# Products that nobody reads, in the gaps of TensorE's program behind the experts

## The reference, cut to what matters

```
h = layernorm(x) * (1 + ca) + sa
x = x + ga * L0_attn(h)      # convolutions, gated delta rule scan, output projection
h = layernorm(x) * (1 + cb) + sb
x = x + gb * L0_ffn(h)       # router, softmax gates over 8 experts of 128 -> 512 -> 128
h = layernorm(x) * (1 + ca') + sa'
x = x + ga' * L1_attn(h)     # in_proj, causal conv, state space scan in chunks, out_proj
h = layernorm(x) * (1 + cb') + sb'
x = x + gb' * L1_ffn(h)      # 128 -> 512, butterfly, gelu, butterfly, 512 -> 128
```

## Time and profile before

| | |
|---|---|
| median of 3 runs | 572.57 us (570.67 to 573.45) |
| profiled execution: its time | 571.0 us |
| its span | 568.9 us |
| PE busy in the span | 445.5 us (78%) |
| ACT / DVE / POOL busy | 392.6 / 376.6 / 193.0 us |
| mean granted clock of TensorE | 0.904 |

### The profile page before, as it was taken

The page is one execution under the profiler, slowest core; times in us unless marked ns, Lnnn a source line. Parts: engine busy times, 40 slices in busy tenths (PEclk is TensorE's granted clock), DMA queues, the critical chain, the costliest instruction groups (busy, mean ns, idle before and its releaser), DMA issues.

```text
span 568.9 us, 6438 instructions
## 1 busy us (share of the span) xinstructions
PE 445.5 (78%) x2064; PEld 303.8 (53%) x2064; DVE 376.6 (66%) x663; ACT 392.6 (69%) x661; POOL 193.0 (34%) x188
## 2 busy tenths in 40 slices
PE   5585597479975777998969989999999889864145
PEld 4474573267654654665746656676656566441012
DVE  1326958698979999799998958999231483022800
ACT  3798747757898558689745997746996676924242
POOL 0150961396108971048791104541003000030001
PEclk9988777978999999899988998999999999985557
DMA  7637537232270311800240081000000000000000
GB/s 204 231 122 180 164 100 300 47 93 75 67 140 1 93 40 56 188 0 1 60 109 0 1 189 38 1 1 1 0 1 20 1 1 1 0 18 0 1 1 18
DMA packets 35473, 36.49 MB, mean 64 GB/s; under 512 B 12904, under 2 KB 30832, under 8 KB 35184
## 3 DMA queue, kind: packets, MB, share of 16 engines
q1 hardware_dynamic: 35152, 31.88, 21.2%
q10 hardware_dynamic: 288, 4.19, 1.9%
HBM read 31.61 MB, written 3.28 MB: 61 GB/s over the span
## 4 chain that ended last, share of the span: by engine, by line
PE 34%; DVE 22%; ACT 16%; POOL 11%; issue 9%; DMA 2%; SPq 2%; POOLq 0%; DVEq 0%; ACTq 0%
PE psF L751 8%; PE psS L769 8%; PE psB L708 4%; DVE XX L1798 3%; DVE norm L1795 3%; DVE U L1815 3%; DVE T L1813 3%; DVE T L1817 3%; PE psM L812 3%; ACT L1086 2%; ACT hid L1280 2%; ACT L1088 2%; ACT hS L1129 2%; PE psM L819 2%; POOL G L2154 2%
## 5 line engine op out<-in xcount | busy, mean ns | idle before, releaser
L769 PEld LDWEIGHTS psS<-we2s,hid 128*128 128x128 f32 x1024 | 136.5, 196 | 61.2 <-issue 46.9
L751 PE MATMUL psF<-h,we1s 128*128 128x512 f32 (+1 forms) x320 | 139.7, 528 | 13.2 <-ACT hid L1280 12.5
L769 PE MATMUL psS<-we2s,hid 128*128 128x128 f32 x1024 | 138.9, 280 | 10.8 <-DVE acc L1836 5.5
L1280 ACT ACTIVATE hid<-psF,col 128x512 f32<-128x512 f32 (+1 forms) x160 | 93.2, 598 | 57.6 <-PE psF L751 56.9
L2203 POOL TENSOR_TENSOR QS<-H,qn 128x512 f32<-128x512 f32 x32 | 44.8, 1414 | 95.3 <-DVE H L1823 86.0
L751 PEld LDWEIGHTS psF<-h,we1s 128*128 128x128 f32 x320 | 54.9, 199 | 41.5 <-ACT hid L1280 22.0
L1836 DVE SCALAR_TENSOR_TENSOR acc<-psS,gate,acc 128x128 f32<-128x128 f32 x128 | 36.3, 340 | 33.7 <-PE psS L769 33.7
L1823 DVE TENSOR_TENSOR_SCAN H<-A,T 128x576 f32<-128x576 f32 x32 | 55.3, 1727 | 1.1
L1088 ACT ACT_TABLE_LOAD x41 | 52.6, 1283 | 0.7
L1813 DVE TENSOR_TENSOR T<-wrep,H 128x648 f32<-128x648 f32 x32 | 33.6, 1050 | 14.3 <-DMA wrep<-XX 13.9
L1815 DVE TENSOR_REDUCE U<-T 128x64 f32<-128x576 f32 x32 | 38.7, 1208 | 1.1
(11 more groups left out here) (193 smaller groups left out, 734.7 us busy)
## 6 DMA issues: line engine op xcount, KB each, us to landing
wrep<-scratch_dram SPq DMA_DIRECT2D x64, 144.0 KB, 3.6
krep<-scratch_dram SPq DMA_DIRECT2D x64, 128.0 KB, 3.0
hid<-fold_mats_dram SPq DMA_DIRECT2D x22, 256.0 KB, 5.2
we1s<-we_dram ACTq DMA_DIRECT2D x1, 2048.0 KB, 7.9
we2s<-we_dram ACTq DMA_DIRECT2D x1, 2048.0 KB, 12.4
wrep<-XX SPq DMA_DIRECT2D x8, 144.0 KB, 3.4
outT_dram<-x SPq DMA_DIRECT2D x4, 256.0 KB, 2.6
scratch_dram<-XX SPq DMA_DIRECT2D x3, 288.0 KB, 2.1
```

Source lines behind the costliest of these rows:

```text
L751: mm(bank[name][:, 0:ncols(w)], we1s[:, e, k * P:(k + 1) * P], h2[w % 2][:, 0:ncols(w)], start=True, stop=True).then_inc(s_hid_mm, 1)
L769: last = mm(bank[name][:, t * P:(t + 1) * P], hid[n % 2][:, k, t * P:(t + 1) * P], we2s[:, e, k, :], start=(k == 0), stop=(k == HT - 1))
L1280: nc.scalar.activation(hid[x_ % 2][:, k, 0:c], psF[n % 2][:, 0:c], ACT.Silu, bias=pc("be1", HT * e + k)).then_inc(s_hid_done, 1)
```

## The change

PE's program gets a helper, `fill(i, n)`, that issues n products of the identity with the first expert's weights (512 columns), in turn into banks F0 and F1. They increment no semaphore and nothing reads the banks afterwards. It is called in five places behind `experts_back(4)`. Nothing else differs, and no other engine's program is touched.

```diff
+            def fill(i, n):
+
+                for j in range(n):
+                    free(f"F{(i + j) % 2}")
+                    mm(psF[(i + j) % 2][:, :], cst("ident"), we1s[:, 0, :], start=True, stop=True)
...
             experts_back(4)
+            fill(0, 1)
             center(("ssd", 3))
             variance(("ssd", 3))
+            fill(1, 4)
             ssd_in(3)
+            fill(5, 13)
             ssd_out(3)
+            fill(18, 1)
             center(("ffn", 3))
             variance(("ffn", 3))
+            fill(19, 4)
             for i in range(0, 4):
                 ffn_up(3, i)
             ffn_down(3)
```

## The result

The changed kernel takes 565.35 us in the median of six runs (561.0 to 571.47), before takes 571.65 in six (568.14 to 576.19). The ratio is 0.9874 with a 95% interval of 0.9833 to 0.9914, so 7.2 us faster (4.9 to 9.5). A second session gave 565.42 us in six runs against 572.72 in eleven, a ratio of 0.9844 (0.9794 to 0.9895).

What follows compares the result with a forecast made beforehand. The tail was taken as bound by one chain of waits through the engines, with TensorE mostly at half clock. Gains of 6.05 us, less 0.4 and 0.35, net 5.3 off 572.57, gave 567.3 us; range 564.6 to 571.0.

Steps and rivals of the forecast that it cites:

- ssd_in 3: Two products of ssd_in in the tail: clock returns during the four fills before them; 1.8 us gained, bounds 0 and 1.8.
- ssd_out 3: Product behind the 13 fills: 4.6 us of rest loses the clock; 0 us gained, bounds 0 and 0.95.
- center ffn 3: Center of ffn 3, behind ssd_out and one fill: clock returns in it or just behind; 0.4 us gained, bounds 0 and 0.95.
- ffn_up, ffn_down: Last products before output: 9.98 us on the chain become 7.5 at full clock; 2.4 us gained, 0 if the clock isn't back.
- late fills: Fills in the second or fifth gap run late and delay the chain; 0.4 us taken off, bounds 0 and 1.7 each.
- other executions: Another execution may have had some true product at full clock before the change too; 0.35 us taken off.
- step 1: Center of ssd 3: one more product delays the clock's fall into center or variance; 0.5 us gained, bounds 0 and 0.95.
- C: Rival: clock holds nearly throughout the tail, also before ssd_out; 8.3 us gained, 564.3 us; chance 0.10.
- A: Rival: clock isn't kept or returns too late in the tail, though fills fit; 1.5 us gained, 571.1 us; chance 0.13.
- term 1: Center of ssd 3: the first fill makes the clock fall some microseconds later; 0.5 us gained, bounds 0 and 0.95.
- B: Rival: unread products don't bring the clock back, fills take 1.71 us and delay the chain; 9.8 us lost, 582.4; chance 0.04.
- D: Rival: about 115 extra PE instructions cost fetching on the chain; 0 to 1 us lost; chance 0.03, shared with something unseen.

Runs made afterwards that it cites:

- second trace: The changed kernel run once more, unaltered, with fills of 1, 4, 13, 1 and 4 products: tail 56.8 us, ratio to before 0.9844.
- the longer fills: Against the changed kernel, fills of 3, 5, 17, 2 and 5 products in place of 1, 4, 13, 1 and 4: 563.05 and 563.25 us.
- the doubled block: Against the changed kernel, 8 products in place of 4 in the second fill, ahead of ssd_in 3: tail 60.1 us, ratio to before 0.9939.

## Why the prediction was right and where it fell short

The mechanism held: the products that nobody reads keep TensorE at full clock through most of the tail, and the true ones on the chain become shorter by what the rows had said. Too little was forecast all the same: 567.3 us, where the five runs that are compared have a median of 564.22. Taken as differences between the starts of successive true products, so that they sum to the tail, the terms came out so:

| term | predicted | first trace | second trace |
|---|---|---|---|
| center ssd 3 | 0.5 | 0.46 | 0.61 |
| variance ssd 3 | 0 | 0 | 0 |
| ssd_in 3 | 1.8 | 1.80 | 1.80 |
| ssd_out 3 | 0 | 0.80 | 0 |
| center ffn 3 | 0.4 | 0.53 | 0.77 |
| variance ffn 3 | 0.95 | 0.95 | 0.95 |
| ffn_up, ffn_down | 2.4 | 2.30 | 2.30 |
| late fills | -0.4 | 0 | 0 |
| other executions | -0.35 | | |
| sum | 5.3 | 6.8 | 6.4 |

The large terms, ssd_in and the ffn products, came out to within 0.1 us. The step that failed is the last one, from the gains to a time and its range. First, the 0.4 us taken off for late fills had no row behind it and measured 0 in both traces. The reasoning that led there was off too. The return was counted from 509.6, though step 1 had the clock still up then; in fact it fell 0.5 us into center (at 517.5 in the first trace) and took 6.8 us to return (at 524.3), longer than the 3 to 5.5 that I had expected, with about two low fills among the block's four, just short of the third that would have made it late. Second, ssd_out and center of ffn 3 were put at 0 and 0.4 and measured 0.80 and 0.53 in the first trace, 0 and 0.77 in the second.

Third, the base. The 572.57 us came from three runs; the six have 571.65. So the 3.1 us between forecast and measured are 0.9 from the base, 1.1 to 1.5 from the terms of the tail, and 0.6 to 1.0 that no trace shows a place for. Last, the lower end of the range, 564.6, was set by one case alone, and even that case (C, 564.3) lay outside it, as did A's 571.1 at the upper end, where the text says that the range holds most of A. The six runs of before span 8 us and those of the change 10; by the starts of L789 that scatter comes from the body, and it belonged into the range on both sides.

The 0.35 us for other executions can't be called wrong. I took it off because before may at times have a true product at full clock, and center of ssd 3 was faster by 0.5 to 0.6 us in the two kernels without a fill ahead of it. By the same two kernels term 1 is right by luck: 0.46 and 0.61 us stand against 0.5, but the cause given for them, that the first fill delays the fall, is not shown.

What the times show beyond the tail, 7.2 and 8.9 us against 6.8 and 6.4, lies inside their intervals.

One reading of the rows was wrong and changed nothing in the sum: the clock row is not at nine tenths "nearly everywhere" before the last five slices, 11 of the 35 read 7 or 8, most of them in the first ten.

ssd_out was rightly bounded: 0.80 in one trace, 0 in the other, in the same kernel after the same rest. The claim that DVE isn't slowed is shown by the scan at 1.22 us, the one that a met wait is free by 13 products in 11.32 us. The rule of the Trainium skill on products that cycle through PSUM banks (TensorE: Matmul & The Clock Gate, "A second HAM failure mode: psum-queue depth-cycling") names short rests between groups of products as the cause. The fills have no such rests, and this case's trace gives no sign of the swing: 17 products in two banks in turn ran at full clock from first to last (14.76 us in the kernel with the longer fills).

Of the rivals, A is out: L812 is at 4.05 us in every version that has the last block of fills on all rows. One sign of B did appear, L796 starting right at the end of a fill; but ACT's last piece ended 0.05 us before it, so the fill cost nothing. B did not happen to the change, but its mechanism is real and only one choice away: with 32 rows its three delays came to 2.1, 3.5 and 2.1 us, where I had priced 1.7, 6.4 and 1.7 (the third block started while the clock was up). C is what the longer fills reach, by 8.7 us where I had written 8.95. Of D no trace shows a sign: true products in front of which the clock was up came out as short as the rows had them.

## What to carry to other kernels

Where the end of a kernel is a chain through all engines and the granted clock of TensorE reads low, products into a bank that nobody reads can hold it up; count what each true product on the chain gains (0.95 us for one of 512 columns in fp32 here), and fill each gap to within a microsecond of its end and not beyond, since all that sticks out delays the chain. Use all 128 rows: fills on 32 rows kept PE busy, didn't bring the clock back, and made the kernel slower. Look first whether the products are on the chain at all; in the body of this kernel the same trick raised the clock and gained nothing. And take more than one trace of the kernel before: some of what a change seems to gain can be there without it.

## What the runs showed of the hardware that was not expected

- Fills on 32 of 128 rows left the granted clock at 0.50 for 37.3 us in which PE was busy for 36.5; fills on all rows with 32 columns of weights, as many and as long, held it at 1.00 but for the two low stretches that the change has too (tail 56.4 us in both).
- The same rest of 4.46 us kept the clock in one execution until 0.9 us into the product behind it, and lost it 2.2 us before that product in another. With the doubled block it was lost 2.4 us before the product. A single trace of such a stretch is one draw.
- At a granted clock of 1.00, back-to-back records of 512 columns followed each other at 0.429 to 0.430 us (median) in 13 traces, and at 0.448 in one execution, the first with fills in the body, from its beginning to its end (530.15, 530.60; timeline of PE's weight loads below). The granted clock does not show the difference, and it wasn't pursued.

```profile
530.15 0.19 PEld L827 LDWEIGHTS psF<-we1s,C 128*128 128x128 f32 x1 [0.26 <-issue]
530.60 0.19 PEld L827 LDWEIGHTS psF<-we1s,C 128*128 128x128 f32 x1 [0.26 <-issue]
```
